# Grouped-query attention rewritten: keys and values made inside the head stream, values weighed per query half, a split output projection, rows normalised at the add to x

## The reference, cut to what matters

```python
def _L1_attn_b_ref(hidden_states, Wq, Wk, Wv, Wo, q_norm_w, k_norm_w):
    q = (hidden_states @ Wq).reshape(b, s, NH, HD)      # 32 heads of 128
    k = (hidden_states @ Wk).reshape(b, s, NKV, HD)     # 4 heads
    v = (hidden_states @ Wv).reshape(b, s, NKV, HD)
    q, k = _rms_norm(q, q_norm_w), _rms_norm(k, k_norm_w)
    q, k = _apply_rope(q, k, cos, sin)
    k, v = jnp.repeat(k, 8, axis=1), jnp.repeat(v, 8, axis=1)
    scores = jnp.where(causal, q @ k.T * scaling, min)
    attn = jax.nn.softmax(scores, axis=-1)
    return (attn @ v).reshape(b, s, NH * HD) @ Wo
...
x = x + _L1_attn_b_ref(_layernorm(x), ...)
```

## Time and profile before

| | |
|---|---|
| runs before, median (lowest, highest) | 2095.08 us (2091.97, 2095.51) |
| profiled execution, span | 2109.5 us |
| PE busy | 1714.7 us, 81% of the span |
| DVE busy | 1329.9 us, 63% |
| ACT busy | 912.2 us, 43% |
| POOL busy | 705.7 us, 33% |
| mean granted clock of TensorE | 0.876 of full speed |
| DMA | mean 46 GB/s |

### The profile page before, as it was taken

How to read it: one execution, slowest core, us unless ns; L and a number is a source line. 1 busy time by engine, 2 the same in 40 slices (tenths; PEclk the granted TensorE clock), 3 DMA queues, 4 the chain that set the end, 5 groups by cost and what they waited for, 6 DMA issues and landing times. The chain is left out here.

```text
span 2109.5 us, 32349 instructions
## 1 busy us (share of the span) xinstructions
PE 1714.7 (81%) x10854; PEld 1377.9 (65%) x10854; DVE 1329.9 (63%) x2578; ACT 912.2 (43%) x1761; POOL 705.7 (33%) x630
## 2 busy tenths in 40 slices
PE   6999788878845552835899999999999999999463
PEld 4434677667722222834788888888888888888353
DVE  3664644763469985445677667776777767774533
ACT  2456343333342322523455455554555545554232
POOL 3011333033357737034433223332333223330512
PEclk9899799879967885867899999999999999999676
DMA  3222332033200004430000000000000000000443
GB/s 79 49 37 79 113 120 84 31 120 108 88 7 0 0 3 157 138 112 3 8 6 9 11 11 2 10 10 10 10 10 7 10 10 2 10 6 6 133 136 107
DMA packets 79122, 97.67 MB, mean 46 GB/s; under 512 B 12064, under 2 KB 63776, under 8 KB 79024
## 3 DMA queue, kind: packets, MB, share of 16 engines
q1 hardware_dynamic: 72880, 79.59, 12.9%
q0 software_dynamic: 6144, 16.79, 2.5%
HBM read 62.25 MB, written 27.66 MB: 43 GB/s over the span
## 5 line engine op out<-in xcount | busy, mean ns | idle before, releaser
L1063 ACT ACTIVATE gqa_probs<-acc,gqa_bias,gqa_q_scale 128x128 f32<-128x128 f32 (+7 forms) x256 | 212.7, 831 | 258.8 <-DVE gqa_bias L1154 258.5
L1322 PE MATMUL aux<-gqa_probsT,gqa_v 128*128 128x128 f32 x2304 | 311.6, 282 | 1.4 <-ACT gqa_oT L1085 1.4
L1150 DVE TENSOR_REDUCE gqa_neg_max<-acc 128x1 f32<-128x128 f32 (+7 forms) x256 | 193.6, 756 | 165.8 <-PE acc L1289 163.3
L1322 PEld LDWEIGHTS aux<-gqa_probsT,gqa_v 128*128 128x128 f32 x2304 | 288.9, 198 | 8.2 <-issue 5.1
L1006 POOL TENSOR_TENSOR gqa_q_high<-gqa_straight,gqa_turned_q 128x512 fp32r<-128x512 f32 x64 | 81.5, 1274 | 510.9 <-DVE gqa_turned_q L1111 510.9
L1306 PE MATMUL aux<-ident,gqa_probs 128*128 128x128 f32 x1152 | 180.7, 280 | 7.6 <-DVE gqa_probsT L1182 4.6
L1342 PE MATMUL acc<-gqa_wo,gqa_oT 128*128 128x256 f32 x512 | 153.5, 427 | 4.8 <-DVE stream L1188 4.8
L1306 PEld LDWEIGHTS aux<-ident,gqa_probs 128*128 128x128 f32 x1152 | 135.9, 144 | 30.3 <-DVE gqa_probsT L1182 14.8
L1288 PE MATMUL acc<-gqa_k_high,gqa_q_high 128*128 128x512 f32 (+3 forms) x384 | 148.0, 385 | 1.0 <-ACT gqa_probs L1063 1.0
L1182 DVE COPY gqa_probsT<-aux 128x128 f32<-128x128 f32 (+3 forms) x256 | 123.0, 481 | 34.9 <-PE aux L1306 33.8
L1288 PE MATMUL acc<-gqa_k_high,gqa_q_low 128*128 128x512 f32 (+3 forms) x384 | 134.9, 351 | 0.0
(11 more groups left out here) (387 smaller groups left out, 4422.5 us busy)
## 6 DMA issues: line engine op xcount, KB each, us to landing
f_w<-in_f_up SPq DMA_DIRECT2D x64, 256.0 KB, 2.8
f_xs<-tokens_by_slot SPq DMA_DIRECT2D x108, 128.0 KB, 2.2
outputs_by_slot<-f_y_tile SPq DMA_DIRECT2D x108, 128.0 KB, 1.7
f_w<-in_f_down SPq DMA_DIRECT2D x64, 128.0 KB, 3.1
mat_qk<-mat_high SPq DMA_DIRECT2D x64, 64.0 KB, 2.3
gqa_w_q<-in_g_wq SPq DMA_DIRECT2D x32, 128.0 KB, 2.0
gqa_wo<-in_g_wo SPq DMA_DIRECT2D x32, 128.0 KB, 2.1
tokens_by_slot<-zeros SPq DMA_DIRECT2D x1, 3968.0 KB, 13.2
```

The source lines that it names most:

```text
L1063: act.activation(probs[:, j % 4, 0:width(j)], scores(j), ACT.Exp, bias=bias[:, j % 16:j % 16 + 1], scale=q_scale[:, j // NT % 2, tile_of(j ...
L1150: dve.tensor_reduce(neg_max[:, j % 16:j % 16 + 1], scores(j), AX, ALU.max, negate=True).then_inc(max_ready, 1)
L1322: last = pe.matmul(aux[:, 2 + t // 4, t % 4 * P:(t % 4 + 1) * P], v[:, g, s, :], probsT[:, j % 4, s * P:(s + 1) * P], start=(s == 0), stop ...
```

## The change

All of it is in `gqa_layer`; the other layers are word for word the same. What it does:

- The heads are taken in their natural order, eight for a group, and the tiles of a head in order of width, 128 to 1024 keys. The hardware loop is gone: the 274 steps are written out.
- Only group 0's keys and values are made ahead. Those of groups 1 to 3 are made in the stream, `kv` in step 7 of the second to fifth head of the group before, `turn_k` in step 7 of the sixth and seventh.
- Exponentials are not scaled. They are transposed as they are, all copies are on ACT, and the inverse of the row sum is applied where the output is added to x (`scalar_tensor_tensor`).
- `weigh` works on half of the queries at once: for keys s, one fp32 product with as many columns as queries of that half that see them (512 to 128), all into bank 2 of `aux`.
- That output is split into high and low parts (`high_oT` on ACT, `low_oT` on DVE), and so is `wo`. `out` is a product in three, one head and two tiles at a time, into the same bank 2 of `aux`.
- The sum of squares is made for two heads at once: four fp32 products of 512 columns with 32 columns of ones as weights, each on 32 partitions of its own, then a copy and four transposes.

```diff
+            def add(h, q):
+                dve.wait_ge(wo_done, 4 * h + q + 1)
+                dve.wait_ge(inv_ready, 2 * h + q // 2 + 1)
+                for t in (2 * q, 2 * q + 1):
+                    dve.scalar_tensor_tensor(core.x[:, t, :], aux[:, 2, t % 2 * D:(t % 2 + 1) * D], row_inv[:, h % 3, t:t + 1],
+                                             core.x[:, t, :], ALU.mult, ALU.add).then_inc(added, 1)
...
+            for n in range(STEPS + TAIL):
+                h, j = divmod(n, NT)
+                if n < STEPS:
+                    row_max(n)
+                if j == 1 and h + 2 < HEADS:
+                    rope(h + 2, 0)
+                if j == 3 and h + 2 < HEADS:
+                    rope(h + 2, 1)
+                if j == 2 and 1 <= h <= HEADS:
+                    low_oT(h - 1, 0)
+                if j == 7 and 1 <= h <= HEADS:
+                    low_oT(h - 1, 1)
...
+                if j == 0 and 0 <= h - 2 < HEADS:
+                    add(h - 2, 3)
+                if j in (2, 3, 7) and 0 <= h - 1 < HEADS:
+                    add(h - 1, (0, 1, 2)[(2, 3, 7).index(j)])
...
+            def sum_squares(p):
+                free(("sum", p, 0))
+                pe.wait_ge(squared, 4 * p + 4)
+                for q in range(4):
+                    last = pe.matmul(aux[32 * q:32 * q + 32, 3, :], ones[:, :], square[:, q // 2, q % 2 * HALF:(q % 2 + 1) * HALF],
+                                     start=True, stop=True)
+                last.then_inc(square_sum, 1)
...
+            def weigh(h, half, keys):
+                if keys[0] == 0:
+                    pe.wait_ge(chunk_copied, CHUNKS_OF_HEAD * h + (CHUNKS_OF_HEAD if half else 4))
+                    if half:
+                        pe.wait_ge(added, NT * h + 4)
+                    elif h >= 1:
+                        pe.wait_ge(added, NT * h)
+                for s in keys:
+                    first, moving = turned_keys(half, s)
+                    last = pe.matmul(aux[:, 2, first:], v[:, h // GQ % 2, s, :], moving, start=s == 0, stop=s == 4 * half + 3)
...
+            def out(h, q):
+                if q % 2 == 0:
+                    pe.wait_ge(oT_low_ready, 2 * h + q // 2 + 1)
+                    pe.wait_ge(wo_low_ready, h + 1)
+                else:
+                    pe.wait_ge(added, NT * h + 2 * q)
+                for t in (2 * q, 2 * q + 1):
+                    rows = slice(t * P, (t + 1) * P)
+                    for m, (a, b) in enumerate(three(oT_high[:, rows], oT_low[:, rows], wo_high[:, h % 2, :], wo_low[:, h % 2, :])):
+                        last = pe.matmul(aux[:, 2, t % 2 * D:(t % 2 + 1) * D], a, b, start=m == 0, stop=m == 2)
+                last.then_inc(wo_done, 1)
...
+            for n in range(STEPS + TAIL):
+                h, j = divmod(n, NT)
+                if n < STEPS:
+                    score(n)
+                if j == 0 and 0 <= h - 2 < HEADS:
+                    out(h - 2, 3)
+                if 0 <= n - TURN < STEPS:
+                    turn(n - TURN)
+                if j in (0, 2) and h + 2 < HEADS:
+                    project(h + 2, j // 2)
+                if 0 <= h - 1 < HEADS:
+                    if j == 1:
+                        weigh(h - 1, 0, (0, 1, 2, 3))
+                    if j == 2:
+                        out(h - 1, 0)
+                    if j == 3:
+                        out(h - 1, 1)
+                    if j == 4:
+                        weigh(h - 1, 1, (0, 1))
+                    if j == 5:
+                        weigh(h - 1, 1, (2, 3))
+                    if j == 6:
+                        weigh(h - 1, 1, (4, 5, 6, 7))
+                    if j == 7:
+                        out(h - 1, 2)
```

More of the change, by code:

```diff
@@ new lines, in turn_sum, with score @@
+            def turn_sum(p):
+                pe.wait_ge(sum_copied, p + 1)
+                for b in range(4):
+                    last = pe.transpose(aux[:, 3, b * P:(b + 1) * P], sums[:, b * P:(b + 1) * P], core.ident[:, :])
+                last.then_inc(sum_turned, 1)
+            def score(n):
+                h, t = divmod(n, NT)
+                g = h // GQ
+                if t == 0:
+                    pe.wait_ge(q_ready, 2 * h + 2)
+                    pe.wait_ge(k_low_ready, 2 * g + 2)
+                if h >= 1 or t >= 4:
+                    pe.wait_ge(exp_done, n - (1, 2, 2, 3, 2, 1, 1, 1)[t])
+                for a in range(0, width(t), HALF):
+                    b = min(width(t), a + HALF)
+                    for m, (left, right) in enumerate(three(q_high[:, h % 3, t * P:(t + 1) * P], q_low[:, h % 3, t * P:(t + 1) * P],
+                                                            k_high[:, g % 2, a:b], k_low[:, g % 2, a:b])):
+                        pe.matmul(scores(t)[:, a:b], left, right, start=m == 0, stop=m == 2 and b < width(t))
+                pe.matmul(scores(t)[:, t * P:(t + 1) * P], ident_b[:, :], below[:, :], start=False, stop=True).then_inc(scored, 1)
@@ new lines, in turn @@
+            def turn(n):
+                t = n % NT
+                pe.wait_ge(exp_done, n + 1)
+                for c, (a, b) in enumerate(parts(t)):
+                    if chunk(n, c) >= 2:
+                        pe.wait_ge(chunk_copied, chunk(n, c) - 1)
+                    elif c == 0:
+                        pe.wait_ge(roped, 4)
+                    for s in range(a, b):
+                        last = pe.transpose(aux[:, chunk(n, c) % 2, (s - a) * P:(s - a + 1) * P], probs_of(t, s, s + 1), core.ident[:, :])
+                    last.then_inc(chunk_turned, 1)
@@ L1345, in _ @@
-            steady(pe, [(4, project), (4, sum_squares), (12, score), (OUT, out), (TURN, turn), (WEIGH, weigh)])
-            for t in range(4):
-                out(STEPS // 32, t)
+            project(0, 0)
+            project(0, 1)
+            for q in range(4):
+                kv(0, q)
+            project(1, 0)
+            project(1, 1)
+            pe.wait_ge(v_copied, 4)
+            turn_k(0, 0)
+            turn_k(0, 1)
+            pe.wait_ge(made, 4)
+            sum_squares(0)
+            turn_sum(0)
```

820 lines of the change are left out of this document (432 added, 388 removed).

## The result

Six runs of the changed kernel took 2098.63 to 2103.57 us, median 2099.55; six of the kernel before 2091.97 to 2096.61, median 2094.49. The ratio is 1.0027 [1.0017, 1.0037] (the bracket is the 95% interval of the ratio): slower, by 5 us, where 52 were forecast.

What follows compares the result with a forecast made beforehand. PE's issue of products was taken to bound the kernel. The stage was 39 + 18 + 31 x 32.4 + 25 = 1086 us in place of 1034, plus 52, giving a median of 2147 us, whole range 2055 to 2205.

Steps and rivals of the forecast that it cites:

- PE bounds the stream: Changed attention stage: the stream ends when PE has issued its products; other engines count only when they make PE wait.
- Work of a head: PE's products in one head at full clock: 26.2 us, plus 0.2 on average for key and value products.
- The eight products of the sum of squares: Eight instructions for two heads, side by side on four partition sets: about 1 us, minus 1.10 us of work.
- The output: Output product in three, 24 products at 0.12 us in a head, 2.8 us in place of 3.68: minus 0.87.
- Weighing: Half of the queries at once: time goes by columns, so no gain; bounds nothing or 0.4 us less a head.
- The four waits: PE waiting for DVE inside a head, walked in order: 0.35, 1.95, 1.75 and 0.9 us, together 4.95 us.
- the two long ones: PE waits 1.95 us before the second half's weighing for the second add, 1.75 before the third output for `low_oT`.
- the two small ones: PE waits 0.35 us before the second output product of a head and 0.9 before the fourth.
- The clock: Granted clock falls about once a head behind the new long waits: 1.05 us a head, bounds 0 and 3.4.
- Rival 1: The clock holds in the stream: a head is 31.35 us, plus 20 us, 2115 us; chance 0.17.
- Heads that are not full: The stream was counted as 31 equal heads of 32.4 us, the first and last intervals included.
- Ends: Outside the 31 heads: 39 us to the first row maximum, 18 for the first head, 25 behind the last scores.

Runs made afterwards that it cites:

- e1: Changed kernel with the second add of a head moved ahead of the query rotation in DVE's order; 2050.8 us, 0.9787 of the kernel before.
- e2: Changed kernel with the second half's low_oT moved ahead of the 1024-key row maximum in DVE's order; 2040.23 us, 0.9733 of the kernel before.
- e3: Changed kernel with both DVE moves, second add ahead of rotation and second-half low_oT ahead of row maximum; 1986.91 us, 0.9492 of before.
- e5: e3 plus first low_oT ahead of its row maximum, first output product ahead of the projection, fourth behind the transposes; 1959.8 us, 0.9357 of before.
- e11: e5 with the output as one fp32 product per tile, a plain copy on ACT and no low_oT; 1967.91 us, 0.9403 of before.
- e13: Changed kernel with an extra unused DVE operation of 128 columns ahead of each head's second add; 2125.13 us.
- e9: Changed kernel with an extra unused DVE operation of 256 columns ahead of each head's second add; 2136.81 us.
- e7: Changed kernel with an extra unused DVE operation of 512 columns ahead of each head's second add; 2151.51 us.
- e4: Kernel before with its sum-of-squares products given 128 columns in place of one (sums not the reference's); 2064.79 us, 0.9855 of before.
- e10: Changed kernel with 16 one-column fp32 products ahead of the sum of squares, 15 times in the stream; 2178.01 us, 1.0409 of before.
- e8: Changed kernel with three extra unused DVE operations of 512 columns ahead of each head's second add; 2292.24 us.
- e14: Changed kernel with an extra DVE operation of 256 columns ahead of the second half's low_oT; 2137.81 us, 1.0218 of before.

## Why the direction was right and the size wrong

- **PE bounds the stream: right.** e1 to e3 give back what waits are taken away, e5 ends at PE's work.
- **Work of a head, 26.4 us: right, 26.55 in e5 with 0.2 of waiting,** but by luck in part, since two terms were off against each other. The eight products of the sum of squares took 1.00 us (1426.71 to 1427.71), as predicted. The output was to save 0.87 us and saved about 0.3 (e11): a set of six takes 0.8 and not 0.70, since its first product takes 0.2. Weighing was taken to gain nothing, with 0.4 us as the other bound, and gained about that: its 24 instructions took 7.75 us in one head of the changed kernel (2.07 + 1.88 + 1.72 + 2.08, starts 1413.68, 1424.83, 1429.26 and 1433.15), where 72 of 128 columns were 8.1. The last eight, of 512, 512, 384, 384, 256, 256, 128 and 128 columns, in the timeline of PE:

```profile
1433.15 2.32 PE L1444 MATMUL aux<-gqa_probsT,gqa_v 128*128 128x512 f32 x8
1435.23 0.47 PE L1420 MATMUL acc<-gqa_k_high,gqa_q_high 128*128 128x512 f32 x1
```

- **The four waits, 4.95 us: their sum nearly right, 4.5,** the two long ones at their places with their releasers; the two small ones were over-estimated, and a fifth of 0.22 us was taken as none. The largest was 1.95 in the walk, from issue to issue, and 1.73 in the trace (1423.10 to 1424.83; the row counts from the transposes' end and says 1.56). PE came to it on time, 4.0 us behind the start of the first output product. DVE was earlier: each pair of adds took 0.79 us to the next operation, not 1.0, though the first began 0.1 us later than walked.
- **The clock, 1.05 us a head: this is the step that failed.** It measured nearly nothing: the granted clock was 0.99 over the stream and 1.00 from 1000 to 1880 us, and a full head took 31.08 us where full clock was to give 31.35. I took a wait of 1.85 us with a fall behind it as the size of the new ones. Had the wait been as long as walked, the term would have been half right: e13, with that wait (1.95 from issue to issue is 1.78 in a row), loses 0.64 us a head, e9 0.9 and e7 1.1. The walk was 0.2 us too long at the one place where 0.2 us is worth 20 us, and the remaining 0.4 us of the term was an overestimate also for the walked wait. Rival 1 had this case, 31.35 us a head at full clock; measured 31.08. It got 0.17, too little. What spoke against it was one wait in another layer, in a stretch in which PE was busy for 2.55 us of 4.40, which the new stream is not; that this is why the clock fell there is not shown.
- **Heads that are not full: a second step that failed, by 17 us.** 31 equal heads were multiplied, but the first interval and the last two are 3 to 5 us shorter than the others (27.6, 25.8, 27.0), together 80.4 us where 3 x 32.4 = 97.2 were counted.
- **Ends: right within 9 us.** To the first row maximum of 1024 keys 59.7 us (57 predicted), behind the last one 30.8 (25).

The sum of the miss: full heads 28 x (32.4 - 31.08) = 37 (clock 29, the rest 8), short heads 17, ends -9, together 45 of the 45 us between 1086 and 1041. The 8 us are the waits, 0.45 us a head shorter than forecast, less 0.15 us more of work. Rival 1 with the short heads counted gives 57 + 28 x 31.35 + 80.4 + 25 = 1040 us for the stage; it measured 1041. So close a sum is luck in part: its ends are 9 us short and its heads 8 us long.

Where the gain went is thus shown. Ahead of the stream some 41 us were saved (first score product at 948.44, 35.7 us after the start of the stage, where 77 us lay ahead of the stream). In a full head PE was spared 28.13 - 26.55 = 1.6 us of work (28.13 is the 28.46 of the earlier trace rows less its wait of 0.33), 1.1 us of clock and the old wait of 0.3, and 4.5 us of waits were paid, most of them for an operation that DVE had behind a rotation or a row maximum: from 29.57 to 31.08 us, 28 times that is 42. (By the row maxima of 1024 keys, the same measure as after, 28 heads of before average 29.28 us, and it is 50.) e5 keeps the first and drops the second, at 0.936 of before.

## What to carry to other kernels

When a bank is passed between two engines inside a loop, look at what stands ahead of the awaited operation in the other engine's list; moving it forward by one place cost nothing that these runs show, and was worth 49 and 59 us here. Whether a second bank in place of the shared one would have done the same was not tried. A term that switches, like the clock, deserves both of its values in the forecast and not the middle, above all when the wait on which it rests is known only to 0.2 us. And multiply by full repetitions only: the first and last ones of a pipeline are shorter.

## What the runs showed of the hardware

- The granted clock fell behind one-column products though the profile shows PE busy over them: 30 us over the stream in the kernel before (e4), 1.6 us each time in e10, there with a wait of 1.56 us just ahead. The Trainium skill (TensorE: Matmul & The Clock Gate, Part 1: The HAM clock gate) ties the clock to how busy PE has been. The waits of e7, e8, e9, e13 and e14 agree with that; that one-column products, with the engine busy in the profile, bring the clock down too can't be read from it.
- The same wait of 1.9 us is followed by a fall in one head and not in the next (e9), so the cost of a wait is a mean over many: 0.6 us at 1.77 us, 2.4 at 5.5.
- DVE is slowed beside POOL. The bias of one column takes 0.16 us in all 169 cases of the changed kernel in which no POOL operation runs beside it; of the 87 beside one 67 take more than 0.5 us, up to 1.24, all of them beside POOL's operations of 512 columns. Its mean rose from 235 to 398 ns. In e8 three operations of the kind that takes 0.69 us in e7 took 4.03 together, while POOL was busy for 4.68 us of 5.50 (timeline of DVE, window of the wait):

```profile
1472.37 4.03 DVE L1336 TENSOR_TENSOR gqa_scratch<-xnT 128x512 f32<-128x512 f32 x3
```

```profile
1471.80:1477.30 5.50, 0.04 (x1) 0.00 (x0) 5.47 (x7) 0.38 (x1) 4.68 (x3) 0.79 0.00 0
```

  The Trainium skill (SBUF — State Buffer, SBUF: two separate sides) has it that a DVE operation with two inputs in SBUF and a POOL operation that reads SBUF lock each other out; these rows agree, but no run here took POOL's work away.
